# A graph and attention kernel with narrower edge windows, folded attention weights, a vectorised expert table and one-hot matrices made one tile at a time

## The chip, the cores and the metric

The kernel runs on one core of a Trainium2 chip. The metric is the device time of one execution in microseconds (us), from start to end. The kernel before takes 4575.36 us (median of 3 runs, 4572.35 to 4579.07). Everything is one program; no host arithmetic happens between its stages.

Names used below: PE is the matrix engine (TensorE), PEld its weight load, DVE the vector engine, ACT the scalar engine, POOL the GpSimd engine, SP the engine that only issues transfers.

## The reference, cut to what matters

A graph of 6250 nodes (256 features) has 106,250 directed edges, sorted by destination; each node also has an edge to itself. Four blocks follow each other on the node features:

```python
x1 = layernorm(x)
h  = segment_sum(x1[src], dst) + eps1 * x1          # graph layer 1, edges gathered: 256 wide
h  = relu(relu(h @ W1a + b1a) @ W1b + b1b)
h  = segment_sum(h[src], dst) + (1 + eps2) * h      # graph layer 2, edges gathered: 512 wide
x  = x + relu(h @ W2a + b2a) @ W2b + b2b
# attention over 64 "slices" per head, 8 heads of 64:
sw = softmax(((ln(x) @ W_x + b_x) @ W_slice + b_slice) / temp)
token = (sw^T @ (ln(x) @ W_fx + b_fx)) / (sum(sw) + 1e-5)
q, k, v = token @ W_q, token @ W_k, token @ W_v     # 64 x 64 weights, shared by the heads
x  = x + (sw @ softmax(q k^T / 8) v) @ W_out + b_out
# graph layer 3: normalised adjacency, 256 wide, batch norm, relu, residual
x  = x + relu(bn(D^-1/2 A D^-1/2 (ln(x) @ W) + b))
# mixture of 8 experts, 2 chosen per node:
x  = x + sum over the chosen e of gate_e * (relu(ln(x) @ W1[e] + b1[e]) @ W2[e] + b2[e])
```

The kernel moves the second graph layer's first product (W2a) in front of the gather, so that 512 columns are gathered there. All arithmetic on the features is in 32-bit floats.

## The kernel before, in words

**Edge tiles.** The nodes lie in NB = 49 blocks of 128. The edges, sorted by destination, are cut into tiles of 128 consecutive edges; four blocks (a unit) share UT = 69 tile columns. Block q of a unit owns the columns q*18 to q*18 + 17 (CAP = 18; q = 3 has 15). Since the edges of a block don't start exactly there, a block also reads the last EARLY[q] tiles of the block before it: EARLY = (0, 2, 4, 5). A tile that holds edges of two blocks is thus multiplied twice, once for each block. Edges that fall outside a block's window of columns go through a slow loop of "spare" tiles, whose tables the first stage makes (lines 541 to 556 and `spare_tiles`). With the inputs of the metric the loop runs once in each layer, its least number.

**One graph layer** runs 846 tile columns in 282 groups of up to GT = 3 tiles. For a group POOL issues one indirect transfer for each tile, which gathers 128 source rows by the indices in `src_idx` (`gather`, line 275). DVE compares the row of 128 node numbers with the tile's destinations, which gives the one-hot matrix of the tile (`compare`, line 289), three tiles in one instruction, and once more for the tiles that the next block also reads (`early`). PE multiplies one-hot and rows and sums in PSUM (`sums`, line 314; for the next block's tiles line 324). PE is told that a group's rows have landed by a semaphore; POOL may start a group when PE has finished the one 8 groups back (layer 1) or 6 groups back (layers 2 and 3): `pool.wait_ge(self.s_used, g - self.SLOTS + 1)`. DVE makes the one-hots a block ahead.

**What else lies in a layer.** `pipeline` (line 185) cuts the dense work on four finished blocks (the two hidden products, layer norm, soft-max, gates) into 22 pieces and puts them between the edge groups of the following four blocks. Each engine runs its own stream in program order; what waits on one engine holds all behind it. `close` takes a block's sums out of PSUM.

**The attention** (stage `s3`) stands between layer 2 and layer 3, with no gather beside it. It is a chain: PE transposes the tokens (L1446), products with W_fx (L1451), DVE assembles the block-diagonal `stok` (L1350, L1354), PE transposes, three products for q, k and v (L1459 to L1461), DVE copies the three (L1361), scores (L1465), soft-max on DVE and ACT (L1367 to L1378), transpose (L1469), product with v (L1473), product with W_out (L1477), copies (L1385, L1386). Then PE starts the long product with the slice weights (L1487).

**The experts** (stage `s5`) start with a table on DVE: from the running counts `run` of nodes per expert, it makes the first tile of each expert, the expert of each of TM = 105 tiles and the node numbers of each tile (`tnode`). All other engines wait for `s_tn`, which comes after eight copies (L2041), each behind a load of its offset into a register. Then 105 tiles run, each with a gather by POOL (L1950), products on PE, and an adding scatter by POOL (L1943).

The lines that the change touches: the constants (line 55), `tiles_of` (98), `dst_l` (210), `compare`, `onehots`, `sums` (287 to 325), the windows (552), `s3` (1263 to 1480), the node numbers of layer 3's placement (1600, 1791, 1799) and the prologue of `s5` (1877 to 2043).

## Time and profile before

| | us |
|---|---|
| median of 3 runs | 4575.36 |
| lowest, highest | 4572.35, 4579.07 |
| the profiled execution, its own time | 4574.74 |
| its span, first to last instruction | 4572.8 |

| engine | busy us | share of the span | instructions |
|---|---|---|---|
| PE | 3460.2 | 76% | 12646 |
| PEld | 2289.5 | 50% | 12648 |
| DVE | 1387.5 | 30% | 3920 |
| ACT | 491.6 | 11% | 1148 |
| POOL | 2855.9 | 62% | 2814 |

The profiled execution takes what the unprofiled ones take: 1.94 us separate its own time from its span. Busy times of PE are modelled (matrix products are pipelined and overlap in the records), so the distance between the starts of following products says more than their durations. The mean granted clock of PE is 0.868 of full speed; the records know two levels, 1.2 and 2.4 GHz. A share over the whole span mixes the stages; the windows further down keep them apart.

### The profile page before, as it was taken

The page shows a single profiled execution, that of the slowest core. Times are in us where ns is not written, and L with a number is a line of the kernel's source. Part 1 is how long each engine was busy: PE and PEld are TensorE (multiplying, and loading weights), DVE is VectorE, ACT ScalarE, POOL GpSimd, SP SyncE. Part 2 cuts the span into 40 slices and gives each one's busy share as a digit, 9 for nine tenths or more (in the row PEclk, how much of TensorE's full clock was granted, in tenths as well). Part 3 has the DMA queues.
Part 4 walks back from the last instruction along what each step waited for, and adds up shares of the span by engine and source line. Part 5 has one row for each costly group of instructions (what it writes and reads, how often), then busy time and mean ns, then how long its engine had stood idle before and what let it go on. Part 6 is the DMA issues. An engine that isn't in the chain of part 4 may idle for free. (4 is left out here: it accounts for less than half of the span.)

```text
span 4572.8 us, 39338 instructions
## 1 busy us (share of the span) xinstructions
PE 3460.2 (76%) x12646; PEld 2289.5 (50%) x12648; DVE 1387.5 (30%) x3920; ACT 491.6 (11%) x1148; POOL 2855.9 (62%) x2814
## 2 busy tenths in 40 slices
PE   3478777877888898989999976566556656648996
PEld 2345444544553444444544545345444444437986
DVE  5111111211121343334333435233333333442221
ACT  4000000100110000000000002000000000003332
POOL 3666666666646676767767502676666767635664
PEclk7789888988999999999999978777777777779998
DMA  5333333433349666666666527334334333327887
GB/s 184 95 108 112 109 112 110 127 111 111 110 122 329 189 189 197 195 187 194 199 196 206 169 90 236 115 115 119 119 113 129 115 112 115 118 64 187 205 209 188
DMA packets 321328, 687.01 MB, mean 150 GB/s; under 512 B 58976, under 2 KB 148300, under 8 KB 320854
## 3 DMA queue, kind: packets, MB, share of 16 engines
q0 software_dynamic: 169712, 474.01, 37.7%
q10 hardware_dynamic: 86448, 110.35, 7.3%
q1 hardware_dynamic: 64970, 100.14, 6.7%
q8 instruction: 107, 1.75, 0.2%
q14 instruction: 91, 0.75, 0.0%
HBM read 592.43 MB, written 99.13 MB: 151 GB/s over the span
## 5 line engine op out<-in xcount | busy, mean ns | idle before, releaser
L275 POOL DMA_INDIRECT s_edge_rows<-table,w_src_idx x2538 | 2558.2, 1008 | 1207.3 <-issue 714.4
L314 PE MATMUL s_psA<-s_edge_rows,s_onehot 128*128 128x257 f32 (+2 forms) x5076 | 1731.7, 483 | 282.7 <-issue 131.1
L314 PEld LDWEIGHTS s_psA<-s_edge_rows,s_onehot 128*128 128x128 f32 x5076 | 1026.7, 207 | 843.4 <-issue 733.0
L289 DVE TENSOR_TENSOR s_onehot<-w_iota_row,w_dst_l 128x384 f32<-128x384 bf16 x846 | 432.2, 552 | 17.3 <-PEq L144 15.5
L324 PE MATMUL s_psA<-s_edge_rows,s_early 128*128 128x257 f32 (+2 forms) x792 | 263.6, 457 | 11.4 <-issue 9.5
L1943 POOL DMA_INDIRECT acc_rows<-s_y,s_tnode x105 | 166.4, 1585 | 128.1 <-DVE s_y L2063 99.8
L968 PE MATMUL s_psM<-s_h1T,s_w1b 128*128 128x512 f32 (+2 forms) x448 | 196.5, 584 | 53.8 <-ACT s_h1T L870 44.6
L974 PE MATMUL s_psM<-s_w2a,s_hT 128*128 128x512 f32 x392 | 198.2, 651 | 31.8 <-ACT s_hT L874 17.8
L2086 PE MATMUL s_psU<-s_xT,s_w 128*128 128x128 f32 x1680 | 208.3, 278 | 0.0
L2086 PEld LDWEIGHTS s_psU<-s_xT,s_w 128*128 128x128 f32 x1680 | 199.3, 195 | 0.1
L2096 PE MATMUL s_psD<-moe_w,s_hT 128*128 x840 | 199.3, 380 | 0.0
L324 PEld LDWEIGHTS s_psA<-s_edge_rows,s_early 128*128 128x128 f32 x792 | 152.6, 193 | 92.9 <-issue 78.4
L1820 PE MATMUL s_psT<-w_ident,s_agg 128*128 128x128 f32 x98 | 27.8, 380 | 203.6 <-DVE s_agg L1719 149.7
L928 DVE SCALAR_TENSOR_TENSOR s_own<-s_psM,s_eps,s_b2a 128x512 f32<-128x512 f32 x49 | 36.8, 751 | 443.4 <-ACT s_trow L880 293.8
L918 DVE TENSOR_TENSOR w_degree<-w_degree,s_psA 128x1 f32<-128x1 f32 x49 | 7.5, 153 | 539.7 <-remote 226.6
L2096 PEld LDWEIGHTS s_psD<-moe_w,s_hT 128*128 128x128 f32 x840 | 152.4, 192 | 16.6
L968 PEld LDWEIGHTS s_psM<-s_h1T,s_w1b 128*128 128x128 f32 x448 | 88.7, 206 | 136.5 <-issue 83.1
L974 PEld LDWEIGHTS s_psM<-s_w2a,s_hT 128*128 128x128 f32 x392 | 81.1, 211 | 121.7 <-issue 100.4
L2000 ACT ACTIVATE s_hT<-s_psU,moe_b 128x128 f32<-128x128 f32 x420 | 119.8, 368 | 169.1 <-issue 96.5
L962 PE MATMUL s_psM<-s_aggT,s_w1a 128*128 128x512 f32 (+2 forms) x224 | 105.5, 614 | 36.8 <-issue 36.8
L1950 POOL DMA_INDIRECT s_xs<-xl_rows,s_tnode x105 | 103.9, 989 | 46.5 <-issue 30.2
L2063 DVE SCALAR_TENSOR_TENSOR s_y<-s_psD,s_part,s_yb 128x256 f32<-128x256 f32 x105 | 50.9, 484 | 269.3 <-PE s_psD L2096 253.6
(352 smaller groups left out, 2771.9 us busy)
## 6 DMA issues: line engine op xcount, KB each, us to landing
s_w<-in_L_ffn_W_dram SPq DMA_DIRECT2D x105, 512.0 KB
s_edge_rows<-table,w_src_idx POOLq DMA_INDIRECT x2538
s_swT<-swt_rows SPq DMA_DIRECT2D x12, 1024.0 KB
table<-s_trow ACTq DMA_DIRECT2D x11, 1024.0 KB
own_rows<-s_own ACTq DMA_DIRECT2D x11, 1024.0 KB
s_self_h<-own_rows ACTq DMA_DIRECT2D x11, 1024.0 KB
swt_rows<-s_swT ACTq DMA_DIRECT2D x11, 1024.0 KB
extra_rows<-w_zeros SPq DMA_DIRECT2D x7, 896.0 KB
```

Of the source, the lines that this page charges most:

```text
L275: pool.indirect_dma_start(self.rows[:, g % self.SLOTS, t, :], None, self.table, bass.IndirectOffsetOnAxis(ap=src_idx[:, at:at + 1], axis=0 ...
L289: return nc.vector.tensor_tensor(into, iota_row[:, q * P:(q + 1) * P].unsqueeze(1).to_broadcast([P, n, P]), dst_l[:, at:at + n].unsqueeze( ...
L314: last = nc.tensor.matmul(banks[b % 2][:, 0:w], self.onehot[:, g % self.AHEAD, t, :], self.rows[:, g % self.SLOTS, t, col:col + w], start= ...
L324: last = nc.tensor.matmul(banks[(b + 1) % 2][:, 0:w], self.early[:, b % 2, i * GT + t - (CAP - max(EARLY)), :], self.rows[:, g % self.SLOT ...
L962: last = mm(psM[m][:, 0:n], w1a[:, c, m * P:(m + 1) * P], aggT[:, c, 0:n], start=c == 0, stop=c == KD - 1)
L968: last = mm(psM[m][:, 0:n], w1b[:, c, m * P:(m + 1) * P], h1T[:, c, 0:n], start=c == 0, stop=c == KH - 1)
L974: last = mm(psM[j][:, :], hT[:, c, j * P:(j + 1) * P], w2a[:, c, :], start=c == 0, stop=c == KH - 1)
L1943: pool.indirect_dma_start(acc_rows, bass.IndirectOffsetOnAxis(ap=tnode[:, t:t + 1], axis=0), y[:, t % 4, :], None, compute_op=ALU.add).the ...
L1950: pool.indirect_dma_start(xs[:, t % RING, :], None, xl3_rows, bass.IndirectOffsetOnAxis(ap=tnode[:, t:t + 1], axis=0)).then_inc(s_xs[t % R ...
L2000: last = ac.activation(hT[:, t % 2, m, :], psU[t % 2][:, m * P:(m + 1) * P], ACT.Relu, bias=b1[:, bass.ds(e, 1), m])
L2086: last = mm(psU[t % 2][:, m * P:(m + 1) * P], w1[:, t % WRING, k, m * P:(m + 1) * P], xT[:, t % 2, k, :], start=k == 0, stop=k == KD - 1)
L2096: last = mm(psD[t % 2][:, 0:D], hT[:, t % 2, k, :], w2[:, bass.ds(e, 1), k, :], start=k == 0, stop=k == KH - 1)
```

## The change

Four edits stand in it.

1. The windows of tile columns: EARLY goes from (0, 2, 4, 5) to (0, 2, 3, 4), and a new tuple LATE = (0, 1, 1, 0) leaves the last tile of blocks 1 and 2 of a unit to the next block alone (`used_of`). The gathers stay as they are; the bounds of the windows in the first stage follow.
2. The one-hots: `dst_l` is kept in 32-bit floats, and `compare` issues one TENSOR_SCALAR for each tile, with the tile's destinations as a scalar for each partition, where it issued one TENSOR_TENSOR for up to three tiles.
3. The attention: W_q and W_k are multiplied with each other, W_v with W_out, before they are needed; the queries, the scores and the mix come from these. `stok` is assembled over whole tiles, ACT takes some of the copies, and the soft-max sum is applied at the end, to the mix.
4. The expert table: prefix sums in three steps, the expert of each tile from a comparison over partitions and one product, the spare node numbers as an offset (`value` in layer 3, one more DVE instruction in each of its 14 ranking pieces), half of the eight copies on ACT, and a separate semaphore `s_ex` for what SP, ACT and PE wait for.

```diff
-UNIT, UT, EARLY = 4, 69, (0, 2, 4, 5)
+UNIT, UT, EARLY, LATE = 4, 69, (0, 2, 3, 4), (0, 1, 1, 0)
...
+def used_of(b, g):
+
+    return tiles_of(b, g) - (LATE[b % UNIT] if b + 1 < NB and g == groups_of(b) - 1 else 0)
...
-        dst_l = W.sb("dst_l", [P, COLS], BF16)
+        dst_l = W.sb("dst_l", [P, COLS])
...
             def compare(self, into, q, at, n):
 
-                return nc.vector.tensor_tensor(into, iota_row[:, q * P:(q + 1) * P].unsqueeze(1).to_broadcast([P, n, P]),
-                                               dst_l[:, at:at + n].unsqueeze(2).to_broadcast([P, n, P]), ALU.is_equal)
+                for t in range(n):
+                    last = nc.vector.tensor_scalar(into[:, t, :], iota_row[:, q * P:(q + 1) * P], dst_l[:, at + t:at + t + 1], None, ALU.is_equal)
+                return last
...
-                g, n, ahead = groups_before(b) + i, tiles_of(b, i), early_of(b, i)
+                g, n, ahead = groups_before(b) + i, used_of(b, i), early_of(b, i)
...
-                pool.memset(stok[:, :, :], 0.0)
+                pool.memset(blocks[:, :, :], 0.0).then_inc(s_clear, 1)
...
+                v.tensor_copy(tokT[:, 0, :], psX[0][:, :]).then_inc(s_tokT, 1)
...
+                ch.link(v.tensor_tensor(stok[:, :, :], stok[:, :, :], psX[2][:, :].rearrange("p (c j) -> p c j", c=KH), ALU.add))
+                v.tensor_tensor(stok[:, :, :], stok[:, :, :], blocks[:, :, :], ALU.mult).then_inc(s_stok, 1)
...
+                dve.wait_ge(s_ex, 2)
+                ch.link(v.tensor_reduce(ssum[:, :], pbd[:, :, :], AX, ALU.add))
+                v.reciprocal(ssum[:, :], ssum[:, :]).then_inc(s_rs, 1)
...
+                for c in range(2):
+                    v.tensor_scalar(mix[:, c, :], psX[1][:, c * D:(c + 1) * D], ssum[:, c:c + 1], None, ALU.mult).then_inc(s_mix, 1)
...
+                for i in range(3):
+                    last = nc.tensor.transpose(psM[0][:, pairs[i]], wbd[:, i, :], ident[:, :])
...
+                mm(psM[1][:, 0:P], wT[:, 0, :], wT[:, 1, :], start=True, stop=True).then_inc(s_wfp, 1)
+                for c in range(KH):
+                    last = mm(psM[2 + c // 2][:, c % 2 * D:(c % 2 + 1) * D], wT[:, 2, :], wout[:, c, :], start=True, stop=True)
...
-                    mm(psX[0][:, pairs[c]], wbd[:, 0, :], stokT[:, c, :], start=True, stop=True)
-                    mm(psX[1][:, pairs[c]], wbd[:, 1, :], stokT[:, c, :], start=True, stop=True)
-                    last = mm(psX[2][:, pairs[c]], stokT[:, c, :], wbd[:, 2, :], start=True, stop=True)
+                    last = mm(psX[1][:, pairs[c]], wqk[:, :], stokT[:, c, :], start=True, stop=True)
...
+                    last = mm(psM[c // 2][:, c % 2 * D:(c % 2 + 1) * D], stokT[:, c, :], wvo[:, c, :], start=True, stop=True)
...
+                    last = mm(psX[0][:, pairs[c]], qT[:, c, :], stokT[:, c, :], start=True, stop=True)
...
+                    last = mm(psX[1 - c // 2][:, c % 2 * D:(c % 2 + 1) * D], pbdT[:, c, :], val[:, c, :], start=True, stop=True)
...
+                        ch.link(v.tensor_tensor(value[:, 0:nb, :], node[:, b0:b0 + nb].unsqueeze(2).to_broadcast([P, nb, 2]),
+                                                lane[:, 0:nb, :], ALU.subtract))
...
+                for e in range(NE // 2):
+                    at = act.value_load(tbase[0:1, e:e + 1], min_val=0, max_val=TM)
+                    ac.activation(tnode[:, bass.ds(at, NB)], psI[:, e * NB:(e + 1) * NB], ACT.Identity, bias=spare[:, 0:1]).then_inc(s_copy, 1)
+                    act.wait_ge(s_copy, e + 1)
+                act.wait_ge(s_ex, 1)
...
-                for e in range(1, NE):
-                    ch.link(v.tensor_tensor(tend[:, e:e + 1], tend[:, e:e + 1], tend[:, e - 1:e], ALU.add))
+                for k, step in enumerate((1, 2, 4)):
+                    ch.link(v.tensor_tensor(upto[:, k + 1, 4:], upto[:, k, 4:], upto[:, k, 4 - step:4 + NE - step], ALU.add))
...
-                for e in range(NE):
-                    at = dve.value_load(tbase[0:1, e:e + 1], min_val=0, max_val=TM)
-                    ch.link(v.tensor_scalar(tnode[:, bass.ds(at, NB)], placed[:, e * NB:(e + 1) * NB], 1.0, None, ALU.subtract))
+                at = [dve.value_load(tbase[0:1, e:e + 1], min_val=0, max_val=TM) for e in range(NE // 2, NE)]
+                dve.wait_ge(s_copy, NE // 2)
+                for e in range(NE // 2, NE):
+                    ch.link(v.tensor_scalar(tnode[:, bass.ds(at[e - NE // 2], NB)], psI[:, e * NB:(e + 1) * NB], spare[:, 0:1], None, ALU.add))
```

PE's program in graph layer 2, over blocks 1 to 3 of the first unit and into the next unit (L1223 is the transpose of a closed block; a row's last number counts equal instructions in a row), before:

```order
L314 MATMUL s_psA<-s_edge_rows,s_onehot 128x512 x9
L324 MATMUL s_psA<-s_edge_rows,s_early 128x512
L314 MATMUL s_psA<-s_edge_rows,s_onehot 128x512 x3
L324 MATMUL s_psA<-s_edge_rows,s_early 128x512 x3
L314 MATMUL s_psA<-s_edge_rows,s_onehot 128x512 x6
L1223 MATMUL s_psT<-w_ident,s_agg 128x128 x4
L314 MATMUL s_psA<-s_edge_rows,s_onehot 128x512 x9
L324 MATMUL s_psA<-s_edge_rows,s_early 128x512 x2
L314 MATMUL s_psA<-s_edge_rows,s_onehot 128x512 x3
L324 MATMUL s_psA<-s_edge_rows,s_early 128x512 x3
```

and now:

```order
L320 MATMUL s_psA<-s_edge_rows,s_onehot 128x512 x11
L330 MATMUL s_psA<-s_edge_rows,s_early 128x512 x3
L320 MATMUL s_psA<-s_edge_rows,s_onehot 128x512 x6
L1229 MATMUL s_psT<-w_ident,s_agg 128x128 x4
L320 MATMUL s_psA<-s_edge_rows,s_onehot 128x512 x9
L330 MATMUL s_psA<-s_edge_rows,s_early 128x512
L320 MATMUL s_psA<-s_edge_rows,s_onehot 128x512 x2
L330 MATMUL s_psA<-s_edge_rows,s_early 128x512 x3
```

In this stretch 39 products of a tile became 35, the transposes stayed: block 1 lost one of its own tiles (12 to 11) and one early tile of the next block (4 to 3), block 2 lost one own tile and one early tile (5 to 4). That is 4 products of 80 in each unit of four blocks.

DVE's one-hots for the same kind of stretch in graph layer 1, before:

```order
L289 TENSOR_TENSOR s_onehot<-w_iota_row,w_dst_l 128x384 x5
L289 TENSOR_TENSOR s_early<-w_iota_row,w_dst_l 128x128
L289 TENSOR_TENSOR s_onehot<-w_iota_row,w_dst_l 128x384
L289 TENSOR_TENSOR s_early<-w_iota_row,w_dst_l 128x384
```

and now:

```order
L295 TENSOR_SCALAR s_onehot<-w_iota_row,w_dst_l 128x128 x17
L295 TENSOR_SCALAR s_early<-w_iota_row,w_dst_l 128x128 x3
```

Eight instructions became twenty, each over 128 columns; nothing else moved between them.

## Rows read from the trace of the kernel before

**Rows 1.** Windows by stage: length, busy (x) of PE, PEld, DVE, ACT, POOL, clock, DMA.

```profile
86.40:1303.60 1217.20, 925.22 (x2952) 581.66 (x2953) 209.05 (x484) 120.79 (x201) 829.94 (x847) 0.87 0.40 114
1351.10:2631.90 1280.80, 1163.17 (x3323) 600.86 (x3324) 465.14 (x956) 94.29 (x152) 881.70 (x847) 0.96 0.68 205
2688.20:2722.50 34.30, 19.92 (x80) 16.50 (x80) 13.13 (x32) 0.42 (x1) 0.98 (x2) 0.60 0.51 184
2825.00:4051.90 1226.90, 743.75 (x2728) 566.36 (x2729) 432.83 (x1483) 37.71 (x106) 849.29 (x847) 0.77 0.41 122
4101.60:4117.00 15.40, 0.00 (x0) 0.00 (x0) 8.17 (x39) 0.00 (x0) 0.65 (x3) 0.59 0.00 0
4117.00:4572.80 455.80, 400.94 (x2730) 367.90 (x2730) 103.09 (x315) 159.96 (x525) 270.29 (x210) 0.95 0.79 198
```

**Rows 2.** POOL's gathers in layers 1, 2, 3: busy us, mean ns | idle, its enders.

```profile
L275 POOL DMA_INDIRECT s_edge_rows<-table,w_src_idx x846 | 829.1, 980 | 431.1 <-issue 241.4 <-remote 114.9 <-POOLq L144 44.3
...
L275 POOL DMA_INDIRECT s_edge_rows<-table,w_src_idx x846 | 880.7, 1041 | 398.9 <-issue 233.9 <-DMA s_edge_rows<-table,w_src_idx 70.4 <-PE s_psA L314 59.8
...
L275 POOL DMA_INDIRECT s_edge_rows<-table,w_src_idx x846 | 848.3, 1003 | 377.3 <-issue 239.2 <-DMA s_swT<-swt_rows 92.9 <-PE s_psA L314 35.9
```

**Rows 3.** Timeline, tile products of PE: start us, us, engine line, xcount.

```profile
2651.18 5.31 PE L314 MATMUL s_psA<-s_edge_rows,s_onehot 128*128 128x512 f32 x12
...
3450.52 1.46 PE L314 MATMUL s_psA<-s_edge_rows,s_onehot 128*128 128x256 f32 x6
...
3477.78 2.77 PE L314 MATMUL s_psA<-s_edge_rows,s_onehot 128*128 128x256 f32 x6
```

**Rows 4.** Groups by line, DVE: one-hots and the nearest TENSOR_SCALARs.

```profile
L289 DVE TENSOR_TENSOR s_onehot<-w_iota_row,w_dst_l 128x384 f32<-128x384 bf16 x846 | 432.2, 552 | 17.3 <-PEq L144 15.5 <-issue 0.9
L289 DVE TENSOR_TENSOR s_early<-w_iota_row,w_dst_l 128x256 f32<-128x256 bf16 (+2 forms) x180 | 80.0, 445 | 13.6 <-remote 13.6
L1798 DVE TENSOR_SCALAR s_at_lane<-s_col,s_lane 128x128 f32<-128x128 f32 x98 | 30.6, 312 | 29.4 <-remote 13.4 <-PE moe_psI L1860 13.3 <-issue 2.2
```

**Rows 5.** Timeline of layer 3, POOL gathers beside DVE instructions.

```profile
3474.20 1.39 DVE L1753 TENSOR_SCALAR s_xl<-s_acc,s_mv,s_rstd 128x256 f32<-128x256 f32 x4
3474.20 0.95 POOL L275 DMA_INDIRECT s_edge_rows<-table,w_src_idx  x1 [0.30 <-issue]
...
3524.27 0.56 DVE L289 TENSOR_TENSOR s_onehot<-w_iota_row,w_dst_l 128x384 f32<-128x384 bf16 x1
3524.32 1.33 POOL L275 DMA_INDIRECT s_edge_rows<-table,w_src_idx  x1 [0.31 <-issue]
...
3628.88 0.48 DVE L1799 TENSOR_SCALAR s_at_tile<-s_col,s_tile,s_node 128x392 f32<-128x392 f32 x1
3629.13 1.05 POOL L275 DMA_INDIRECT s_edge_rows<-table,w_src_idx  x1 [0.30 <-issue]
```

**Rows 6.** Timeline of the attention chain.

```profile
2700.39 0.80 PE L1459 MATMUL s_psX<-s_stokT,y_wbd 128*128 128x128 f32 x2 [0.78 <-DVE s_stokT L1357]
...
2708.79 0.86 DVE L1367 TENSOR_SCALAR s_score<-s_psX 64x256 f32<-64x256 f32 x2 [1.37 <-PE s_psX L1465]
...
2712.62 1.11 PE L1469 MATMUL s_psX<-w_ident,s_pbd 128*128 128x128 f32 x4 [3.87 <-DVE s_pbd L1378]
...
2714.52 2.08 PE L1473 MATMUL s_psX<-s_pbdT,s_val 128*128 128x128 f32 x8 [0.78 <-DVE s_pbdT L1381]
...
2717.38 3.78 PE L1477 MATMUL s_psX<-y_wout,s_osT 128*128 128x256 f32 x8 [0.78 <-DVE s_osT L1383]
...
2722.54 9.67 PE L1487 MATMUL s_psM<-s_mix,s_swT 128*128 128x256 f32 x37 [1.38 <-DVE s_mix L1386]
```

**Rows 7.** Timeline, end of the expert table and the first expert gather.

```profile
4109.93 0.19 DVE L2041 TENSOR_SCALAR s_tnode<-s_placed 128x49 f32 x1 [0.48 <-issue]
4110.88 0.19 DVE L2041 TENSOR_SCALAR s_tnode<-s_placed 128x49 f32 x1 [0.76 <-DVE s_tnode L2041]
...
4117.04 0.96 POOL L1950 DMA_INDIRECT s_xs<-xl_rows,s_tnode  x1 [14.79 <-DVEq L2042]
```

More of the change, by code:

```diff
@@ L1376, in _ @@
+                dve.wait_ge(s_scp, 1)
+                own = [psX[0][h * HD:(h + 1) * HD, :].rearrange("p (c j) -> p c j", c=KH)[:, :, h * HD:(h + 1) * HD] for h in range(2)]
                 for h in range(2):
                     rows = slice(h * HD, (h + 1) * HD)
-                    last = v.tensor_tensor(pbd[rows, :, rows], score[rows, :, :], ssum[rows, :].unsqueeze(2).to_broadcast([HD, KH, HD]), ALU.mult)
-                last.then_inc(s_at, 1)
-                dve.wait_ge(s_pe, 6)
-                v.tensor_copy(pbdT[:, :, :], psX[1][:, :].rearrange("p (c j) -> p c j", c=KH)).then_inc(s_at, 1)
@@ L1382, in _ @@
-                dve.wait_ge(s_pe, 7)
-                v.tensor_copy(osT[:, :, :], psX[0][:, :].rearrange("p (c j) -> p c j", c=KH)).then_inc(s_at, 1)
-                dve.wait_ge(s_pe, 8)
-                v.tensor_copy(mix[:, 0:2, :], psX[1][:, :].rearrange("p (c j) -> p c j", c=2))
-                v.tensor_copy(mix[:, 2:4, :], psX[2][:, :].rearrange("p (c j) -> p c j", c=2)).then_inc(s_at, 1)
+                    last = v.tensor_reduce(smax[rows, :], own[h], AX, ALU.max)
+                ch.link(last)
@@ new lines, in _ @@
+                for h in range(2):
+                    rows = slice(h * HD, (h + 1) * HD)
+                    v.tensor_tensor(score[rows, :, :], own[h], smax[rows, :].unsqueeze(2).to_broadcast([HD, KH, HD]),
+                                    ALU.subtract).then_inc(s_sc, 1)
+                dve.wait_ge(s_ex, 2)
+                ch.link(v.tensor_reduce(ssum[:, :], pbd[:, :, :], AX, ALU.add))
+                v.reciprocal(ssum[:, :], ssum[:, :]).then_inc(s_rs, 1)
+                dve.wait_ge(s_pp, 1)
@@ L1468, in _ @@
+                pe.wait_ge(s_q, 1)
                 for c in range(KH):
[L1469 to L1471 removed]
+                    last = mm(psX[0][:, pairs[c]], qT[:, c, :], stokT[:, c, :], start=True, stop=True)
+                last.then_inc(s_scp, 1)
+                pe.wait_ge(s_ex, 2)
                 for c in range(KH):
[L1473 removed]
@@ L2036, in _ @@
[L2036 to L2041 removed]
+                v.memset(upto[:, :, 0:4], 0.0)
```

212 lines of the change are left out of this document (119 added, 93 removed).

## The prediction

> **What bounds the kernel now.** I read first the windows by stage [rows 1]. Five stretches carry the time: three graph layers of 1217, 1281 and 1227 us, the attention chain of 34 us, the experts with 15 us of table and 456 us of tiles. The reader is to see that the layers differ: in layer 2 PE is busy 1163 of 1281 us at a clock of 0.96, so PE sets the pace; in layers 1 and 3 PE is busy 925 and 744 us at 0.87 and 0.77, and POOL 830 and 849 us.
>
> Then POOL's gathers by layer [rows 2]. Undisturbed, a gather takes 0.95 us and the next starts 0.30 us later [rows 5]. 846 gathers at 1.25 us are 1058 us, the floor that POOL sets in each layer. Two things come on top. First, time beyond 0.953 us inside the gathers: 829.1 - 846 x 0.953 = 22.9 us in layer 1, 74.5 in layer 2, 42.1 in layer 3. Second, waits of POOL that are not its own issue gap: 431.1 - 241.4 - 44.3 (the start) = 145 us in layer 1, 398.9 - 233.9 = 165 in layer 2, 377.3 - 239.2 = 138 in layer 3. Whatever name they bear, the only thing a gather waits for is that PE has finished an older group. So in layers 1 and 3 POOL keeps its own pace for most of the time and is held back by PE for some 11 to 12% of it; they set the pace in turns.
>
> Then the collisions [rows 5], the view on which the one-hot edit rests. A one-hot TENSOR_TENSOR starts at 3524.27 and ends at 3524.83; the gather that starts at 3524.32 takes 1.33 instead of 0.95 us. Ended 0.51 us behind the gather's start, it cost 0.38 us: a gather needs something at about 0.13 us after its start that a TENSOR_TENSOR with two inputs in SBUF keeps from it until it ends. A TENSOR_SCALAR train over 256 columns from 3474.20 on costs the gather beside it nothing; one over 392 columns costs 0.10 us (1.05).
>
> **The change part by part.**
>
> *Tile products.* Each unit of four blocks has 69 own and 11 early products, now 67 and 9. Over a layer: 12 units x (2 own + 2 early) = 48 of 978. Twelve records are six products at 512 columns and take 5.31 us, 0.885 us for one; at 256 columns six records are three products in 1.46 us, 0.43 us each after taking off the 0.17 us by which the last record overlaps, and 0.86 us at the low clock (2.77 us) [rows 3]. Layer 2: 48 x 0.885 = 42 us of PE. PE has 9% of idle time there, so I let 40 through; bounds 20 (half absorbed by waits that stay) and 45. Layer 1: 48 x 0.43 / 0.87 = 24 us of PE; layer 3: 48 x 0.43 / 0.77 = 27 us.
> The narrower windows could bring more turns of the spare loop. Counted from the input's edge list, one tile (block 42) now falls outside; the loop ran once before as its least number, and runs once now. Cost 0.
>
> *One-hots.* Removed: 846 + 180 TENSOR_TENSORs, 512 us of DVE [rows 4]. Added: (822 + 108) x 3 = 2790 TENSOR_SCALARs over 128 columns. The nearest row is L1798, 312 ns at 128 columns. By the others a column counts for less: 1.39 / 4 = 0.35 us at 256 and 0.48 at 392 [rows 5], which drawn on to 128 columns gives 0.23. So they take 642 to 870 us, and DVE gains 130 to 358 us of work over 3725 us of layers. DVE is busy 209, 465 and 433 us there [rows 1], so that hides; it would cost where DVE's chain (layer norm, then a block's sums) is what PE waits for. There a train of 5 or 6 one-hots (2.8 to 3.3 us) becomes 15 to 18 (3.5 to 5.6 us), once a unit: at most 12 x 2.3 = 28 us in a layer if nothing hid it. I take 0, since one-hots are made a block ahead.
> What goes is the collision. In layer 1 the one-hots are DVE's only instruction with both inputs in SBUF that recurs, so its 22.9 us are theirs; their number is the same in every layer, so I take 23 us in each. What comes in its place: the 392-column form cost 0.10 us in the row; a third of its columns, near 0. I take 20 of 23 us of POOL's time as gone in each layer.
>
> *What of this reaches the end.* Layer 2: PE paces, the 20 us of POOL bring nothing: 40. Layers 1 and 3: PE gives 24 and 27, POOL 20 and 20; they pace in turns, and relief of one is partly turned into a wait for the other. I take half of the sum: 22 and 23 us. Bounds: 0 (each relief is swallowed by the other) and the whole sum (44 and 47), which could only be passed if PE's arrears vanished.
>
> *Attention.* Span 34.3 us [rows 1]. From the start of q, k, v (2700.39) to the scores' end (2708.79 less 0.05) the chain took 8.4 us: twelve products and three copies. Now four products (a third of 5.1 us: 1.7), then the values' four at 256 columns (3.78 us like L1477), then four scores (1.3): 6.8, gain 1.6. Soft-max to the transposes took 3.8 us; without the separate scaling, with the two halves overlapping ACT's exponential, and with the sum taken later, about 2.2: gain 1.6. From the products with v to the start of the long product 2722.54 - 2714.52 = 8.0 us; now four products at 256 columns (3.8) and two pairs of copies side by side (0.9): gain 3.3. One token copy runs beside the other: 0.6. Against it, W_v x W_out (3.8 us) and W_q x W_k (0.4) lie on PE while DVE assembles `stok` in 1.4 us where 3.3 were needed: a loss of 0.9. Sum 6.2 us [rows 6]; bounds 2 and 10.
>
> *Expert table.* The first gather starts 15.4 us after the stage begins. The eight copies come every 0.94 us [rows 7], 7.1 us from the first to the last. Now ACT makes four (say 1.05 us each) beside DVE's table and its four register loads, then DVE makes four at about 0.2. By that: table 1.8 us, ACT's four until 6.0, DVE's four until 7.0, gather at about 7.9. Gain 7.5 us; bounds 3 and 10. The `value` instruction adds 14 x 0.2 us on DVE, of which the last ones (0.4 us) are on the path.
>
> Sum: 22 + 40 + 23 + 6.2 + 7.5 - 0.4 = 98 us. The profiled execution took 4574.7, 0.6 below the median of the runs: 4574.7 - 98 = 4476.5, near enough **4477**.
>
> **The rivals.**
>
> *A: TENSOR_SCALAR locks POOL out for its whole length.* Each of 930 in a layer takes 0.28 us (between the 0.23 and 0.31 above), 260 us; a gather is at work for 0.95 of each 1.25 us, so 198 us of POOL's time would go. Layer 1: 1058 + 198 = 1256 against 1217, +39. Layer 3: 1058 + 198 + 42 - 23 = 1275 against 1227, +48. Layer 2: 1058 + 198 + 74 - 23 = 1307 against 1281, +26. Less the 13 of the two chains: +100, **4675**. It decides the sign from about 0.15 us for each instruction on. For it: the 1.05 us row. Against it: the 3474.20 train beside a gather of 0.95, and that L1798, of the same shape as the new ones, lies in [rows 2]'s layer 3, whose excess over layer 1 (19 us) its 98 pairs with L1799 can't pass. Chance 0.07.
> The Trainium skill, "SBUF — State Buffer", section "Who interferes with whom", states this as a rule: a TENSOR_SCALAR can enter a mode that takes both port pairs and then holds the pair shared with GpSimd until it ends, while a TENSOR_TENSOR only stands against GpSimd's reads. By that rule the change trades a small collision for a full one. The trace agrees with its second half (1.33 us) and shows of the first only 0.10 us.
>
> *B: the two reliefs add up.* POOL's waits shrink with PE's arrears, DVE never matters: 44 + 45 + 47 + 13 = 149, **4426**. For it: 145 and 138 us of waits are there to be won. Against it: PE's work shrinks by 5% only. Chance 0.15.
>
> *C: PE's clock gives it back.* In layers 1 and 3 the clock is 0.87 and 0.77 where PE has idle time, 0.96 where it has little [rows 1]; a product costs 0.86 instead of 0.43 us at the lower level [rows 3]. If less work makes it idle more and fall more often, layers 1 and 3 bring 0 and layer 2 brings 25: 38 in all, **4537**. Chance 0.13.
>
> *D: DVE's chain becomes late* (28 us in each of layers 1 and 3, a little more in layer 2, against the gains of 40 and 13): about **4590**, and no gain. Chance 0.03.
>
> **How the numbers follow.** Forecast 0.62, A 0.07, B 0.15, C 0.13, D 0.03. What can be told from no change is 0.2%, 9 us. The forecast, B and C lie all below 4566: 0.90. A and the worse half of D are slower: 0.08; the rest, 0.02, within 0.2%. The forecast's own bounds: 98 - 22 - 20 - 23 and more would be the sum of all lower ends, too unlikely together; layers 1 and 3 at 10 each to 35 each give 4505 to 4452. The range takes in B and C: **4425 to 4545**.
>
> **What would show it.** Right: layer 2's length down by about 40 us with PE still busy over 90%; the mean of its products unchanged; in layer 1 a mean gather near 957 ns instead of 980, in layer 3 near 980 instead of 1003; POOL's waits other than issue down from 145 and 138 to about 125; DVE's one-hots at 2790 instructions and under 870 us; the attention chain at 28 us; the first expert gather 8 us after its stage begins. Wrong: gathers with a mean over 1.03 us in layer 1 (A); clocks of layers 1 and 3 below 0.85 and 0.74 with their lengths unchanged (C); PE waiting for `s_onehot` or `s_agg` longer than before (D); more than one spare gather in a layer.

## The result, and the profile after

On the chip of the forecast the changed kernel takes 4554.47 us (median of 7; 4549.62 to 4561.21) against 4572.35 us of the kernel before: ratio 0.996, interval [0.995, 0.997]. It is faster by 18 us where 98 were forecast, and above the forecast's range of 4425 to 4545.

Windows by stage of the changed kernel: length, busy (x) of PE, PEld, DVE, ACT, POOL, clock, DMA. They stand in the order of [rows 1], without the experts: three layers, with the attention behind the second and the table last.

```profile
84.20:1301.10 1216.90, 917.65 (x2870) 578.01 (x2871) 242.26 (x1075) 120.62 (x202) 812.82 (x847) 0.86 0.40 114
1346.00:2623.00 1277.00, 1142.59 (x3227) 594.29 (x3228) 500.95 (x1543) 95.12 (x151) 858.89 (x847) 0.94 0.68 206
2679.20:2701.40 22.20, 16.84 (x78) 14.07 (x78) 9.80 (x19) 5.31 (x11) 0.96 (x2) 0.73 0.79 285
2804.80:4035.80 1231.00, 736.44 (x2631) 551.97 (x2632) 471.33 (x2090) 37.59 (x106) 823.38 (x847) 0.77 0.41 121
4085.80:4093.50 7.70, 0.38 (x2) 0.09 (x2) 3.73 (x21) 1.21 (x4) 0.68 (x3) 0.66 0.30 74
```

The attention fell from 34.3 to 22.2 us and the table from 15.4 to 7.7: 20 us, the whole gain. The layers stand where they stood (1217, 1277, 1231 against 1217, 1281, 1227), although what was to shorten them did happen. POOL's gathers of the changed kernel by layer, as in [rows 2]:

```profile
L280 POOL DMA_INDIRECT s_edge_rows<-table,w_src_idx x846 | 812.0, 960 | 446.3 <-issue 238.8 <-remote 124.8 <-POOLq L149 42.6
...
L280 POOL DMA_INDIRECT s_edge_rows<-table,w_src_idx x846 | 858.1, 1014 | 418.0 <-issue 235.3 <-DMA s_edge_rows<-table,w_src_idx 95.7 <-PE s_psA L320 61.0
...
L280 POOL DMA_INDIRECT s_edge_rows<-table,w_src_idx x846 | 822.5, 972 | 407.4 <-issue 242.2 <-DMA s_spare_dst<-dst_pad 125.4 <-PE s_psA L320 29.5
```

The collisions shrank (mean gather 960, 1014, 972 ns; before 980, 1041, 1003) by 17 to 26 us a layer, and PE is busy 21 us less in layer 2. What was saved came back as idle time in front of the gathers: 446.3, 418.0 and 407.4 us against 431.1, 398.9 and 377.3. The one-hots take 296 ns each, within the 230 to 312 ns of the forecast (here those of the own tiles in all three layers; the early ones are the rest of the 2790):

```profile
L295 DVE TENSOR_SCALAR s_onehot<-w_iota_row,w_dst_l 128x128 f32<-128x128 bf16 x2466 | 531.6, 296 | 28.9 <-PEq L149 15.6
```

### The profile page after: what moved, and what is told of

Its sections match the earlier page's. It is cut to its first block and busy times, and to the rows that moved or that the text cites. A ratio compares the mean times of both kernels' runs of the same rounds, so it can differ in the third digit from the quotient of the medians.

```text
span 4553.2 us, 40537 instructions
## 1 busy us (share of the span) xinstructions
PE 3420.3 (75%) x12357; PEld 2262.4 (50%) x12359; DVE 1485.9 (33%) x5675; ACT 497.9 (11%) x1162; POOL 2790.0 (61%) x2814
## 5 line engine op out<-in xcount | busy, mean ns | idle before, releaser
L280 POOL DMA_INDIRECT s_edge_rows<-table,w_src_idx x2538 | 2492.6, 982 | 1271.7 <-issue 716.2
L320 PE MATMUL s_psA<-s_edge_rows,s_onehot 128*128 128x257 f32 (+2 forms) x4932 | 1692.5, 487 | 200.1 <-DMA s_edge_rows<-table,w_src_idx 101.1
L320 PEld LDWEIGHTS s_psA<-s_edge_rows,s_onehot 128*128 128x128 f32 x4932 | 1015.0, 210 | 748.6 <-issue 622.6
L295 DVE TENSOR_SCALAR s_onehot<-w_iota_row,w_dst_l 128x128 f32<-128x128 bf16 x2466 | 531.6, 296 | 28.9 <-PEq L149 15.6
L330 PE MATMUL s_psA<-s_edge_rows,s_early 128*128 128x257 f32 (+2 forms) x648 | 224.0, 472 | 13.9 <-issue 11.9
L974 PE MATMUL s_psM<-s_h1T,s_w1b 128*128 128x512 f32 (+2 forms) x448 | 186.5, 560 | 7.5 <-issue 6.2
L1910 PE MATMUL moe_psI<-s_at_tile,s_at_lane 128*128 128x392 f32 x196 | 111.1, 702 | 103.2 <-DVE s_at_tile L1849 95.8
L330 PEld LDWEIGHTS s_psA<-s_edge_rows,s_early 128*128 128x128 f32 x648 | 130.4, 202 | 85.2 <-issue 71.0
```

The source lines that it names most:

```text
L280: pool.indirect_dma_start(self.rows[:, g % self.SLOTS, t, :], None, self.table, bass.IndirectOffsetOnAxis(ap=src_idx[:, at:at + 1], axis=0 ...
L295: last = nc.vector.tensor_scalar(into[:, t, :], iota_row[:, q * P:(q + 1) * P], dst_l[:, at + t:at + t + 1], None, ALU.is_equal)
L320: last = nc.tensor.matmul(banks[b % 2][:, 0:w], self.onehot[:, g % self.AHEAD, t, :], self.rows[:, g % self.SLOTS, t, col:col + w], start= ...
L330: last = nc.tensor.matmul(banks[(b + 1) % 2][:, 0:w], self.early[:, b % 2, i * GT + t - (CAP - max(EARLY)), :], self.rows[:, g % self.SLOT ...
L974: last = mm(psM[m][:, 0:n], w1b[:, c, m * P:(m + 1) * P], h1T[:, c, 0:n], start=c == 0, stop=c == KH - 1)
L1910: mm(psI[:, 0:SLOT_TILES], at_lane[:, (2 * b + i) % 4, :], at_tile[:, (2 * b + i) % 4, :], start=False, stop=False, skip_group_check=True) ...
```

## What the trace of before shows when it is read again

The rows of PE, ACT, DVE and POOL around one place of layer 2 of the kernel before. PE's transposes of `s_prob` (L1255) end at 1770.97; ACT's copy of them (L1108) waits for their semaphore alone, and ACT had been idle since 1766.86.

```profile
1770.37 0.60 PE L1255 MATMUL s_psT<-w_ident,s_prob 128*128 128x128 f32 x4
1770.81 1.90 PE L1259 MATMUL s_psM<-s_xl,s_prob 128*128 128x257 f32 x8
1772.54 7.89 PE L314 MATMUL s_psA<-s_edge_rows,s_onehot 128*128 128x512 f32 x18
...
1766.26 0.60 ACT L1108 ACTIVATE s_swT<-s_psT 128x512 f32<-128x512 f32 x1 [4.10 <-issue]
1780.74 0.60 ACT L1108 ACTIVATE s_swT<-s_psT 128x512 f32<-128x512 f32 x1 [13.88 <-DMA x_xl<-in_x_dram]
...
1784.27 0.42 DVE L1205 TENSOR_TENSOR w_tok<-w_tok,s_psM 128x257 f32<-128x257 f32 x1 [26.16 <-DMA table<-x_xl]
1785.00 1.09 DVE L1205 TENSOR_TENSOR w_tok<-w_tok,s_psM 128x257 f32<-128x257 f32 x3 [0.31 <-DMA table<-x_xl]
...
1780.62 0.95 POOL L275 DMA_INDIRECT s_edge_rows<-table,w_src_idx  x1 [0.30 <-issue]
1785.40 0.95 POOL L275 DMA_INDIRECT s_edge_rows<-table,w_src_idx  x1 [3.83 <-DMA s_edge_rows<-table,w_src_idx]
```

ACT starts 9.8 us after the transposes, DVE's additions 11.6 us after the products they wait for (L1259, over at 1772.71), and POOL, which waits for a group of L314, starts at 1785.40, at least 4.97 us after the group had ended (the last of the 18 records is over at 1780.43). The names in the brackets are of no use here (a DMA that had long landed): that the releaser is wrong is the hint. The semaphore updates in the trace say the same: PE's arrive at 1780.7 (the transposes), at 1784.2 (the first of the four products), and then six more within 1.1 us. I call an update of a semaphore that a matmul raises late when no matmul that raises any semaphore has its recorded end within 0.2 us of it. Of the 383, 452 and 451 updates recorded in the three layers of before, 230, 173 and 223 are late; of the stalls of POOL over 0.1 us, 126 of 130 us in layer 1, 91 of 141 in layer 2 and 115 of 120 in layer 3 lie behind the recorded end of the group that the gather waits for; in layers 1 and 3 half of these gathers start over 11 us behind it. It is almost PE's signals alone: by the same test, against DVE's own ends, 3 of DVE's 1485 updates in these layers are late (66 of 1414 in the changed kernel). About a fifth of PE's updates of this trace is not recorded at all (1286 of 1591), which bears on the counts, not on the starts of the other engines.

## The experiments

The layers below run from the first to the last start of a gather; "stalls" are POOL's idle time over 0.3 us before a gather; "late" is as above, over the three layers. Layers, stalls and late updates come from one traced execution each, and traces of the same code differ by up to 7 us in a layer where signals are on time and by up to 16 us where they are late. A session is a set of runs made together on one chip; a figure behind a kernel's name begins a new one and is what the kernel before took there. The rows from "slots 10, 6, 8" to "half of the signals" are kernels without the one-hot edit, the three before "changed (4176)" with 6, 4 and 4 slots.

| kernel | ratio to before | layers 1, 2, 3, us | stalls, us | late |
|---|---|---|---|---|
| before (4572) | 1 | 1216, 1280, 1226 | 131, 143, 121 | 626 of 1286 |
| changed | 0.996 [0.995, 0.997] | 1216, 1276, 1230 | 148, 162, 151 | 719 of 1334 |
| windows only (4536) | 0.9992 [0.9979, 1.0005] | 1204, 1259, 1211 | 126, 126, 116 | 746 of 1327 |
| one-hots only | 0.9987 [0.9977, 0.9997] | 1208, 1251, 1217 | 139, 135, 134 | 743 of 1344 |
| attention and table only | 0.9962 [0.9949, 0.9975] | 1212, 1264, 1211 | 133, 135, 113 | 615 of 1336 |
| all but one-hots | 0.9956 [0.9943, 0.9968] | 1202, 1265, 1212 | 125, 132, 111 | 715 of 1347 |
| slots 10, 6, 8 (4563) | 0.9961 [0.9950, 0.9973] | 1216, 1262, 1221 | 130, 131, 119 | 739 of 1308 |
| slots 6, 4, 4 | 0.9922 [0.9891, 0.9953] | 1217, 1282, 1219 | 136, 154, 122 | 614 of 1294 |
| a third of the products | 0.9812 [0.9786, 0.9839] | 1206, 1244, 1211 | 121, 118, 111 | 608 of 1219 |
| a third of both | 0.6477 [0.646, 0.6493] | 652, 824, 650 | 280, 439, 270 | 6 of 1501 |
| slots 4, 4, 4 (4177) | 0.9979 [0.9968, 0.9989] | 1086, 1185, 1094 | 5, 64, 1 | 0 of 1608 |
| 32 columns set after each gather | 1.0000 [0.999, 1.0011] | 1082, 1197, 1098 | 0, 52, 1 | 0 of 1608 |
| 1024 columns set after each group | 1.1469 [1.1448, 1.149] | 1310, 1356, 1334 | 0, 9, 0 | 0 of 1612 |
| half of the signals | 1.0172 [1.0157, 1.0188] | 1081, 1270, 1101 | 2, 152, 4 | 0 of 1208 |
| changed (4176) | 0.9795 [0.9782, 0.9809] | 1073, 1140, 1080 | 1, 17, 1 | 0 of 1604 |
| windows only | 0.9935 [0.9922, 0.9949] | 1084, 1141, 1092 | 1, 16, 1 | 0 of 1604 |
| one-hots only | 0.9922 [0.9908, 0.9935] | 1070, 1169, 1079 | 1, 53, 2 | 0 of 1602 |
| all but one-hots | 0.9903 [0.9889, 0.9917] | 1081, 1146, 1097 | 1, 17, 1 | 0 of 1604 |
| before (4174) | 0.9999 [0.9988, 1.0009] | 1083, 1164, 1098 | 1, 28, 1 | 0 of 1604 |
| changed, slots 6, 6, 4 | 0.9799 [0.9786, 0.9813] | 1071, 1133, 1077 | 1, 19, 3 | 0 of 1604 |

**The parts, each alone.** Windows alone on the kernel before:

```diff
+UNIT, UT, EARLY, LATE = 4, 69, (0, 2, 3, 4), (0, 1, 1, 0)
+                g, n, ahead = groups_before(b) + i, used_of(b, i), early_of(b, i)
```

> Only the windows change (EARLY 0,2,3,4 and LATE): 48 tile products fewer in a layer, the one-hots still TENSOR_TENSORs, attention and table as before. Theory 1 (two effects that cancel: fewer products help, the longer one-hot trains on DVE take it back): 35 to 60 us below the kernel before, with layer 2 near 1240 us from its first to its last gather. Theory 2 (a layer's length follows neither PE's total nor POOL's own time; a stall once or so in a block refills whatever is saved): within 8 us of the kernel before, layers 1216, 1278 and 1226 us. The forecast on record (products and collisions each count): about 65 us below.

One-hots alone:

```diff
+        dst_l = W.sb("dst_l", [P, COLS])
+                for t in range(n):
+                    last = nc.vector.tensor_scalar(into[:, t, :], iota_row[:, q * P:(q + 1) * P], dst_l[:, at + t:at + t + 1], None, ALU.is_equal)
```

> Only the one-hots as TENSOR_SCALARs with float32 destinations. Theory 1: 35 to 60 us above the kernel before, PE's waits for what DVE hands it in layer 3 (s_at_tile, 29 us before) near 100 us. Theory 2: within 8 us of it although the gathers lose some 20 us a layer of collisions. The forecast on record: about 20 us below.

The changed kernel without both (EARLY back to 0, 2, 4, 5 and LATE to zeros, `compare` back to one TENSOR_TENSOR):

> Only the attention and the expert table as changed; windows and one-hots as in the kernel before. From the trace after, attention takes 22.2 instead of 34.3 us and the table 7.7 instead of 15.4: both theories say 18 to 21 us below the kernel before, as much as the whole change. The forecast on record said 13 for these two.

The changed kernel with only `compare` and `dst_l` back:

> The changed kernel with the one-hots made by TENSOR_TENSOR again: windows, attention and table. Theory 1: 55 to 80 us below the kernel before, and so the best of all. Theory 2: 15 to 25 us below, like the changed kernel. The forecast on record: about 78 us below.

Theory 2 fits all four, and the cancelling of two effects falls: 5, 6, 17 and 20 us below the kernel before (17 is just under the 18 to 21 expected). The gain is that of attention and table, 0.4%; windows and one-hots bring 0.1% each. The kernel before has no trace on that chip; the version with attention and table only has its layers unchanged, and against its 1212, 1264 and 1211 us the windows stand at 1204, 1259 and 1211 and the one-hots at 1208, 1251 and 1217.

**Room and products.** Slots in the call of `Edges`, on the kernel without the one-hot edit (then 6, 4, 4 in the same place):

```diff
-            edges = Edges(S, table1, T1_W, ((0, D + 1),), FP32, GPB - 1)
+            edges = Edges(S, table1, T1_W, ((0, D + 1),), FP32, GPB - 1, slots=10)
```

> Changed kernel without its one-hot edit (that one ran 0.4% below the kernel before), with room for 10 gathered groups instead of 8 in layer 1 and 8 instead of 6 in layer 3; layer 2 keeps 6. POOL's stalls there are some 50 in a layer of 2.5 us each, and the record has PE done with the group in question 5 to 20 us earlier. Theory 'late release' (PE's release reaches POOL late by a bounded time): two more groups are 7.5 us more room, more than nearly every stall, so layers 1 and 3 fall from 1205 and 1212 us to about 1100 each, 200 us less in all. Theory 'common pace' (something that POOL and PE share lets through one gather in 1.43 us whatever the room): layers 1 and 3 stay within 10 us, and the stalls only come later.

> The same kernel with room for 6, 4 and 4 groups instead of 8, 6 and 6. Theory 'late release': the stalls grow by up to 7.5 us each, layers 1 and 3 longer by 150 us and more. Theory 'common pace': layers 1 and 3 longer by less than 30 us.

```diff
-                for t in range(n):
+                for t in range(1):
```

> The same kernel, but PE multiplies only the first of the three tiles of each group (two thirds of the own products are left out; gathers and one-hots stay): PE's tile work falls from 750 to about 330 us in layer 1 and from 1135 to 480 us in layer 2. If PE's work is what POOL waits for, the three layers fall to POOL's own 1060 to 1090 us each, about 430 us less in all. Theory 'late release': layer 2 falls, since PE is its pace; layers 1 and 3 keep at least two thirds of their stalls (80 us each) if the lateness has nothing to do with the products.

```diff
-                        for t in range(tiles_of(b, i)):
+                        for t in range(1):
```

> The same kernel with one gather and one product for each group of three tiles (two thirds of the gathers and own products are left out). POOL's own time falls to 282 x 1.25 = 353 us in a layer. What remains is the pace of the rest (matrix work of PE for each block, DVE's chain, stores): if that is near 1200 us, the gathers were never the bound; both theories expect 500 to 800 us for a layer, with few stalls of POOL that are not its own pace.

Neither room nor PE's work moves layers 1 and 3 by more than 10 us. Layer 1 takes 1216 us with ten slots and 1217 with six; with eight it took 1216 in the first session. With a third of the products PE is busy 806 instead of 1123 us in layer 2, and the layer falls by 17 us against the run with the same 6 slots there (window and gathers of POOL in that run):

```profile
1332.00:2577.30 1245.30, 805.57 (x2174) 425.56 (x2175) 458.27 (x944) 94.50 (x152) 871.33 (x847) 0.79 0.68 211
...
L280 POOL DMA_INDIRECT s_edge_rows<-table,w_src_idx x846 | 870.5, 1029 | 373.9 <-issue 244.1 <-DMA s_edge_rows<-table,w_src_idx 91.6 <-PE s_psA L319 24.2
```

So on that chip PE's work does not pace layer 2 either: 318 us less of it bring 17, and the 1245 us are POOL's 871.3 + 244.1 and some 130 us of waits. And my 'late release by a bounded time' is wrong too: with two groups more of room the same 130 us are paid. A reading that fits, and that no run shows apart: many signals stay away while POOL goes on gathering, and POOL goes on until its room is full. Over half of all late updates (in before 355 of 626) arrive in pauses of POOL over 0.7 us, which are 11 to 12% of the time, most in the last 0.3 us before the next gather.

The run with a third of both differs from the run before it in the gathers alone, on the same chip: 6 of 1501 updates late instead of 608 of 1219. Its layers take 652, 824 and 650 us, the middle one just above the 500 to 800 expected, and the waits in them (280, 439 and 270 us) are not the few that were expected, but nearly all of them end 0.3 us behind PE's recorded end of a group. The fewer slots ran 0.8% below the kernel before; half of that is attention and table again. The rest came from the ends, against the run with 10, 6 and 8 slots: from the last gather of layer 2 to the attention 49.6 instead of 56.7 us, behind layer 3 41.8 instead of 57.2; the layers themselves are 19 us longer. There are two executions of it only.

**Pauses and signals.** On the kernel with 6, 4, 4 slots. These four ran on a chip where the kernel before takes 4177 us.

> Windows, attention and table as changed, one-hots by TENSOR_TENSOR, and room for 4 gathered groups in each layer (8, 6, 6 in the kernel before; 6, 4, 4 ran 0.8% below it). In the runs so far PE's signals stay away while POOL gathers without a break and come in a burst 2 to 4 us after it has stopped, and the stalls of POOL add up to 120 to 135 us in layers 1 and 3 with 10, 8, 6 and 4 slots alike. Theory 'POOL must pause' (the sum of its pauses is fixed, whoever causes them): layer 1 stays within 15 us of 1217 us, and the ends of the layers are a few us shorter: 0.7 to 1.1% below the kernel before. Rival 'room' (4 groups are too few to cover PE's work for a block): layer 1 longer by 50 us and more.

```diff
+                            pool.memset(self.rest[n_rest % 6][:, :], 0.0).then_inc(self.s_rest, 1)
```

> The kernel with 6, 4 and 4 slots, and behind each gather POOL sets 32 columns of a tile that nobody reads (some 0.1 us, and perhaps a gap as long again; 2538 of them, 100 to 250 us in a layer in all). Theory 'POOL must pause' with any break counting: the stalls of 120 to 135 us a layer go and the layers stay within 30 us of 1217, 1282 and 1219 us. With only a long break counting (2 us and more without a gather): the stalls stay, and the layers grow by the full 85 to 250 us. Rival 'PE is late': as the second.

> The same, with one longer break behind each group of three gathers instead: POOL sets 1024 columns of bfloat16 (0.5 to 1 us, 282 in a layer: 140 to 280 us). If a break of that length lets PE's signals through, POOL's other waits fall from 125 to under 40 us a layer and the layers grow by less than 150 us; if not, the waits stay above 100 us and the layers grow by the whole 140 to 280 us.

```diff
-                last.then_inc(self.s_used, 1)
+                if i % 2 or i == groups_of(b) - 1:
+                    last.then_inc(self.s_used, 1 + i % 2)
```

> The kernel with 6, 4 and 4 slots, where PE signals the use of groups only at every second group (by 2) and at a block's end. If what costs is each signal of PE (some 1 in 5 us), half of the group signals make the stalls of POOL fewer: their sum falls from 125 toward 80 us a layer and the kernel by 50 to 120 us. Theory 'POOL must pause': no change of the sum beyond 15 us a layer (with 4 slots and signals for two groups at once, up to 30 us more).

No signal is late there, so none of the four could show what it was made for; they stay inconclusive on it. They do show this. A set of 32 columns (143 ns) behind each gather costs nothing in layers 1 and 3: the gaps between gathers are 0.30 us, and layer 1 takes 1082 us with 846 sets in them. One of 1024 columns behind each group takes 0.97 us and costs 0.80 us in layer 1 (1310 against 1086 us for 282 of them) and 0.85 in layer 3. Layer 2 pays for less room (1185 us with 4 slots, 1146 with 6 in the next session) and for signals at every second group (1270).

**The parts where the signals are on time.**

> The changed kernel once more. Where PE's signals are on time (kernel before near 4177 us): layers 1 and 3 at POOL's own pace lose their collisions (20 us each), layer 2, which PE paces, 40 us, attention and table 19 us: about 100 us or 2.4% below the kernel before, as forecast. Where they are late (kernel before at 4530 to 4575 us): 0.4% below, as measured first.

> Only the windows. Signals on time: layer 2 shorter by 40 us (48 products of 0.885 us), layers 1 and 3 unchanged, since POOL paces them: 0.8 to 1.0% below the kernel before. Signals late: within 0.2% of it.

> Only the one-hots. Signals on time: layers 1 and 3 shorter by 17 to 23 us each (mean gather near 957 ns instead of 980 to 1003), layer 2 unchanged or some us longer (PE paces it and waits for DVE): 0.8 to 1.0% below the kernel before. Signals late: within 0.2% of it.

> Windows, attention and table, one-hots by TENSOR_TENSOR. Signals on time: 40 + 19 us, 1.2 to 1.5% below the kernel before, and so behind the whole change. Signals late: 0.4% below.

> The kernel before, once more with its trace. Signals on time (near 4177 us): layers near 1085, 1169 and 1093 us, of which the excess over 1.255 us for each gather is POOL's collisions (25 to 35 us), and no stall of POOL in layers 1 and 3. Signals late: 1215, 1270 and 1225 us with stalls of 120 to 160 us a layer.

```diff
+            edges = Edges(S, table1, T1_W, ((0, D + 1),), FP32, GPB - 1, slots=6)
+            edges = Edges(S, table3, D, ((0, D),), FP32, 1, slots=4)
```

> The changed kernel with 6 slots in layer 1 and 4 in layer 3 instead of 8 and 6; layer 2 keeps its 6. Signals on time: 2.0 to 2.2% below the kernel before, level with the changed kernel (POOL paces layers 1 and 3 whatever the room). Signals late: 0.5 to 0.8% below, ahead of the changed kernel's 0.4%.

Here the change brings 2.05%, 86 us. Each of the three parts falls short of what was expected of it: windows 0.65% (0.8 to 1.0), one-hots 0.78% (0.8 to 1.0), all but one-hots 0.97% (1.2 to 1.5), the whole 2.05% (2.4); only the version with 6, 6 and 4 slots met its 2.0 to 2.2. The kernel before in such a session, the same place as above: each copy of ACT starts as its transposes end, 4.7 us apart.

```profile
1478.26 0.60 PE L1255 MATMUL s_psT<-w_ident,s_prob 128*128 128x128 f32 x4
1483.00 0.60 PE L1255 MATMUL s_psT<-w_ident,s_prob 128*128 128x128 f32 x4
...
1478.89 0.60 ACT L1108 ACTIVATE s_swT<-s_psT 128x512 f32<-128x512 f32 x1 [4.10 <-PE s_psT L1255]
1483.64 0.60 ACT L1108 ACTIVATE s_swT<-s_psT 128x512 f32<-128x512 f32 x1 [4.15 <-PE s_psT L1255]
```

Windows of the three layers and POOL's gathers in them, the kernel before on this chip:

```profile
78.90:1163.20 1084.30, 907.69 (x3005) 584.87 (x3006) 211.39 (x490) 125.06 (x207) 826.46 (x847) 0.94 0.45 128
1197.40:2362.80 1165.40, 1130.81 (x3316) 587.71 (x3317) 468.02 (x956) 94.18 (x151) 880.72 (x847) 0.99 0.74 225
2557.90:3656.50 1098.60, 709.86 (x2742) 525.18 (x2742) 441.08 (x1506) 37.79 (x106) 840.75 (x847) 0.90 0.46 136
...
L275 POOL DMA_INDIRECT s_edge_rows<-table,w_src_idx x846 | 825.6, 976 | 293.7 <-issue 247.4 <-POOLq L144 36.2 <-PE s_psA L314 6.7
L275 POOL DMA_INDIRECT s_edge_rows<-table,w_src_idx x846 | 879.8, 1040 | 284.6 <-issue 243.4 <-PE s_psA L314 22.5 <-PE s_psA L324 18.7
L275 POOL DMA_INDIRECT s_edge_rows<-table,w_src_idx x846 | 839.9, 993 | 257.6 <-issue 252.1 <-PE s_psA L324 2.7 <-PE s_psA L314 2.7
```

And the changed kernel where its signals are on time:

```profile
78.20:1152.50 1074.30, 881.89 (x2911) 563.02 (x2912) 243.00 (x1076) 125.30 (x208) 816.55 (x847) 0.94 0.45 130
1186.30:2327.50 1141.20, 1094.28 (x3219) 569.67 (x3220) 499.90 (x1544) 94.20 (x151) 867.27 (x847) 0.99 0.75 230
2511.70:3592.70 1081.00, 701.11 (x2646) 514.21 (x2646) 473.47 (x2107) 38.13 (x106) 823.22 (x847) 0.88 0.47 138
...
L280 POOL DMA_INDIRECT s_edge_rows<-table,w_src_idx x846 | 815.7, 964 | 293.6 <-issue 253.1 <-POOLq L149 36.2 <-PE s_psA L320 4.3
L280 POOL DMA_INDIRECT s_edge_rows<-table,w_src_idx x846 | 866.4, 1024 | 273.8 <-issue 250.0 <-PE s_psA L320 15.6 <-PE s_psA L330 8.1
L280 POOL DMA_INDIRECT s_edge_rows<-table,w_src_idx x846 | 822.3, 972 | 257.5 <-issue 250.4 <-PE s_psA L320 5.5 <-PE s_psA L330 1.5
```

Layers 1 and 3 are nothing but POOL: 825.6 + 247.4 and 839.9 + 252.1 of 1084 and 1099 us, and the names behind the arrows now fit. There the windows bring nothing clear (1084 against 1083 in layer 1, 1092 against 1098 in layer 3, but 1080 with them against 1079 without in layer 3 of the kernels with the new one-hots) and the one-hots 10 to 13 and 18 to 19 us. Layer 2 is mostly PE's: windows alone bring 23 us, one-hots alone none (1169 against 1164), while POOL's stalls grow from 28 to 53 us. The version with 6, 6 and 4 slots is level with the changed kernel (0.9799 and 0.9795); where signals are late it was not run.

What the one-hot edit did to the collisions can be read gather by gather. In the first session's traces 343 gathers of the kernel before have one of its one-hot TENSOR_TENSORs at work 0.13 us after their start, and they take 81 us more in all than at 0.953 us each. In the changed kernel 396 gathers meet a one-hot TENSOR_SCALAR there, and those take 16 us more. So the TENSOR_SCALAR holds a gather as well: in 87 of 175 cases in which it had begun before the gather, the gather ends 0.82 to 0.84 us behind the TENSOR_SCALAR's end, as it does behind a TENSOR_TENSOR's (239 of 260); the other cases show little or no delay. One place in layer 2 of the changed kernel, where a train of six ends 0.25 us behind the start of a gather:

```profile
2119.77 1.26 DVE L295 TENSOR_SCALAR s_onehot<-w_iota_row,w_dst_l 128x128 f32<-128x128 bf16 x6
...
2120.78 1.07 POOL L280 DMA_INDIRECT s_edge_rows<-table,w_src_idx  x1 [0.30 <-issue]
```

The edit gains because each instruction is short (0.30 us against 0.55), so that little of it is left at that point, and not because its form spares the gathers.

## Why the prediction was wrong

The step that failed stands in its second paragraph: "Whatever name they bear, the only thing a gather waits for is that PE has finished an older group", and from it "they set the pace in turns". A gather waits for PE's signal, and in three of the six sessions, this one among them, PE's recorded end of the group lies 3 to 20 us before the gather's start in four of five of the waits in layers 1 and 3. The 145, 165 and 138 us of POOL's waits were for the most part no arrears of PE (of the stalls, 126 of 130 us in layer 1, 91 of 141 in layer 2, 115 of 120 in layer 3 lie behind that end), so relief of PE could not shorten them; and relief of POOL only came back as idle time before the gathers. The layers brought 0 of the 85 us forecast for them. The 40 us of layer 2 rested on the first paragraph as well, "so PE sets the pace", read from 1163 busy of 1281 us; with 318 us less of PE's work such a layer fell by 17, about as much as two traces of the same code differ.

Point by point, with what the runs gave where the signals are on time:

- *Tile products, layer 2, 40 us.* The 48 products are gone (PE busy 1131 to 1094 us, 37 less, against 42 worked out), and the layer falls by 24. POOL's own 866.4 + 250.0 = 1116 us stand just under the 1141, so I read it that PE is no longer alone at the pace; no run tests this apart. I had bounded the term by PE's idle time and not by POOL's floor, which was in my own text for the other layers. Where signals are late: 4 us.
- *Tile products, layers 1 and 3.* 24 and 27 us of PE, of which I passed on half; on time they bring 0 to 6, late about 0.
- *Collisions, 20 us.* 825.6 to 815.7 and 839.9 to 822.3 us of gathers, so 10 and 18, and all of it reaches the end on time. The mean gather came to 960 and 972 ns (964 and 972 on time), forecast 957 and 980. Some 5 to 8 us a layer stay, of which I had allowed 3: the new instructions hold gathers too.
- *Attention, 6.2 us.* 12 in all four sessions that have both forms. Two terms were too small. From the start of q, k, v to the scores' end the chain takes 3.8 us where I had 6.8: the values' four products take 1.89 us and not 3.78. And what lies before it was to bring 0.6 less 0.9 and brought 2.5 us: W_v x W_out takes 1.89 us, not 3.8. The clock of the stretch rose from 0.60 to 0.73; I had priced these products at the lower level. Soft-max (1.5 for 1.6 us) and the end (3.3 for 3.3) came out.
  The products of that stretch in the changed kernel (start, us; queries, values, the soft-max's transposes):

```profile
2688.83 1.16 PE L1503 MATMUL s_psX<-s_stokT,s_wqk 128*128 128x128 f32 x8 [0.78 <-DVE s_stokT L1379]
2689.83 1.89 PE L1507 MATMUL s_psM<-s_wvo,s_stokT 128*128 128x256 f32 x8
2694.96 0.66 PE L1516 MATMUL s_psX<-w_ident,s_pbd 128*128 128x128 f32 x4 [2.35 <-ACT s_pbd L1451]
```

- *Expert table, 7.5 us.* 7.7.
- *Rival A* (a TENSOR_SCALAR locks POOL out for its whole length): the price fell. 930 of them in layer 1 and a mean gather of 960 ns; locked out at every moment of each, it would be above the 1.03 us that the forecast names. What the gathers show is a hold at one point near their start, and there the TENSOR_SCALAR can do it too.
- *Rival B* has no case: on time 52 us came from the layers, not 136. *Rival C* (the clock): layers 1 and 3 kept 0.86 and 0.77; no. *Rival D* (DVE's chain): in the first session PE waits longer for DVE's `s_at_tile`, 96 instead of 31 us over the trace, but with late signals DVE itself waits for PE, and on time the same wait is 3 us in both kernels.

That 86 us where signals are on time lie near 98 is in part luck. The layers brought 52 of 85 us, attention and table 20 instead of 13, and 14 us are in no trace: the two traced executions lie 64 us apart, as that of the changed kernel was the slowest of its five (4105 against a median of 4091). For POOL the mechanism was right; in layers 1 and 3 "in turns" was not: there POOL's relief counts in full and PE's for little or nothing.

## What stays open

Why the signals are late in three of six sessions was not found. The runs show that it goes with dense gathers (608 of 1219 updates late with 846 gathers a layer, 6 of 1501 with 282, on one chip), that neither slots nor products change its price, and that it is absent in three sessions on three chips. Each chip was used in one session, and the three late ones came first, so whether it belongs to the chip, to the hour or to what else ran beside it can't be told. Nor can a late signal be told from a product that truly ends late: the ends of matmuls in a trace are modelled. That the next 18 products start 0.44 us apart behind the transposes above speaks for the signal. Whether a break of POOL of a given length ends it was put to a session that does not have it. The windows have no gain under it that can be told from none (interval up to 1.0005); that of the one-hots, 0.13%, is just clear of 1.

## What to carry to other kernels

Before pricing a wait by the work of the engine that releases it, put the releaser's recorded end beside the start of the one released; where microseconds lie between them, or the bracket names a DMA that had long landed, saved work of that engine may bring nothing. Test a bound by cutting its work to a third and by more room: what moves by neither is something else. When an instruction of another form seems to avoid a collision, look at the moment at which it collides: here the shorter length did it. And a result of one session holds for that session: the same edits were worth 0.4% in one and 2.05% in another on another chip, so a gain that the mechanism supports should be timed in more than one.
